# Constant-tile matrix products in TensorE's waits of the first batch, written to a PSUM bank that nobody reads

## The reference, cut to what matters

```python
n = _ln_c(x)                                   # normalise each pixel over the channels
value, query = dwconv(n, w_v), dwconv(n, w_q)  # 3x3 depthwise, stride 1
key, off     = dwconv(n, w_k, 2), dwconv(n, w_off1, 2)
pos  = tanh(gelu(layernorm(off)) @ w_off2 + ref)
v_s  = grid_sample_bilinear(value, pos)        # 784 samples per batch
attn = einsum('bcm,bcn->bmn', query, key) * SCALE
x    = x + einsum('bchw,oc->bohw', einsum('bmn,bcn->bcm', attn, v_s), w_out)
t    = tokens(x)
t    = t + sum_e gate_e(t) * (gelu(_ln_t(t) @ w1[e] + b1[e]) @ w2[e] + b2[e])   # two best of four experts
```

## Time and profile before

| what | value |
|---|---|
| median of three runs | 738.1 us (738.0, 738.1, 743.66) |
| the profiled execution | 742.88 us, span 741.0 us from first to last instruction |
| mean granted TensorE clock | 0.975 of full |
| busy: PE, DVE, ACT, POOL | 696.9, 577.5, 385.4, 216.1 us |
| the chain that ended last | PE 62%, DMA 13%, POOL 10%, ACT 6%, DVE 5% |

### The profile page before, as it was taken

One profiled execution on the slowest core, in us unless ns is written; L12 is line 12 of the kernel. 1 busy time (PEld: TensorE's weight loads), 2 busy tenths in 40 slices (PEclk: granted clock), 3 DMA queues, 4 the chain that ended last, 5 costly groups with the idle time before them and its releaser, 6 DMA issues.

```text
span 741.0 us, 9747 instructions
## 1 busy us (share of the span) xinstructions
PE 696.9 (94%) x3250; PEld 487.7 (66%) x3250; DVE 577.5 (78%) x1511; ACT 385.4 (52%) x722; POOL 216.1 (29%) x184
## 2 busy tenths in 40 slices
PE   5798998899999999899999899999998999999996
PEld 5556566566676666566766566666665665888884
DVE  4899548899999767799998277899984375677774
ACT  2313125654554626644556217544543256999995
POOL 4001700011228500111157200221285121344443
PEclk9997999799999999999999899999999999999998
DMA  9007200134565421354644522344745201121211
GB/s 191 19 0 200 55 8 1 40 70 90 99 180 118 99 48 19 69 110 102 170 120 76 95 48 47 73 86 87 206 104 109 40 25 45 47 75 48 65 47 38
DMA packets 29697, 58.71 MB, mean 79 GB/s; under 512 B 6128, under 2 KB 20176, under 8 KB 29360
## 3 DMA queue, kind: packets, MB, share of 16 engines
q0 software_dynamic: 11584, 17.90, 15.6%
q1 hardware_dynamic: 14336, 32.64, 15.2%
q10 hardware_dynamic: 3728, 7.55, 3.2%
HBM read 30.35 MB, written 14.65 MB: 61 GB/s over the span
## 4 chain that ended last, share of the span: by engine, by line
PE 62%; DMA 13%; POOL 10%; ACT 6%; DVE 5%; issue 4%; POOLq 0%; ACTq 0%
PE py L746 13%; PE pd L662 8%; POOL big L1469 8%; DMA xbuf<-ye 8%; PE ph L578 7%; PE ph L762 3%; PE ph L764 3%; PE ph L763 3%; DMA value_table<-valT 3%; PE pa L650 3%; PE pa L529 2%; PE ph L782 2%; PE ph L784 2%; PE ph L783 2%; PE py L794 2%
## 5 line engine op out<-in xcount | busy, mean ns | idle before, releaser
L746 PE MATMUL py<-hid,w 128*96 128x448 f32 x504 | 235.0, 547 | 12.3 <-ACT hid L1006 9.0
L1006 ACT ACTIVATE hid<-ph,b 128x448 f32<-128x448 f32 x252 | 159.2, 634 | 143.5 <-PE ph L764 138.9
L762 PE MATMUL ph<-x_hi,w_hi 96*128 96x448 f32 x252 | 165.2, 655 | 0.0
L1480 POOL DMA_DIRECT2D xbuf<-ye x76 | 67.6, 889 | 327.3 <-DMA xbuf<-ye 173.4
L1469 POOL DMA_INDIRECT big<-value_table,rows x64 | 85.8, 1340 | 87.0 <-DVE rows L1193 55.2
L746 PEld LDWEIGHTS py<-hid,w 128*96 128x96 f32 x504 | 81.4, 164 | 31.6 <-ACT hid L1006 13.2
L764 PE MATMUL ph<-x_hi,w_lo 96*128 96x448 f32 x252 | 93.4, 371 | 0.0
L763 PE MATMUL ph<-x_lo,w_hi 96*128 96x448 f32 x252 | 92.7, 368 | 0.0
L1416 DVE SCALAR_TENSOR_TENSOR ye<-py,b,gate_all 96x448 f32<-96x448 f32 x112 | 75.4, 675 | 11.7 <-PE py L746 6.5
L1482 POOL TENSOR_TENSOR xbuf<-xbuf,ye 96x448 f32<-96x448 f32 x36 | 54.2, 1506 | 98.9 <-DVE ye L1416 96.2
L1443 DVE TENSOR_TENSOR hid_lo<-hid,hid_hi 128x448 fp32r<-128x448 f32 x84 | 59.5, 709 | 27.8 <-ACT hid L1015 27.4
(11 more groups left out here) (165 smaller groups left out, 1052.7 us busy)
## 6 DMA issues: line engine op xcount, KB each, us to landing
gate_all<-gate_rows SPq DMA_DIRECT2D x56, 336.0 KB, 3.4
xbuf<-ye POOLq DMA_DIRECT2D x76, 168.0 KB, 3.4
value_table<-valT ACTq DMA_DIRECT2D x6, 1176.0 KB, 8.1
out<-xbuf SPq DMA_DIRECT2D x28, 168.0 KB, 2.0
xbuf<-in_x SPq DMA_DIRECT2D x3, 1176.0 KB, 10.5
value_table<-valT SPq DMA_DIRECT2D x2, 672.0 KB, 5.3
big<-value_table,rows POOLq DMA_INDIRECT x64, 2.8
value_table<-valT SPq DMA_DIRECT2D x2, 504.0 KB, 4.4
```

The lines of the kernel that those rows point to most:

```text
L746: nc.tensor.matmul(py[e % 2][0:C, 0:GPIX], w2[:, c, :], hid[:, k % 3, :], start=(j == 0), stop=(j == CPE - 1)).then_inc(hid_used, 1)
L762: nc.tensor.matmul(bank, w1_hi[:, cols], xh(b, g), start=True, stop=False)
L1006: nc.scalar.activation(hid[:, k % 3, :], ph[k % 2][:, 0:GPIX], ACT.Gelu, bias=b1[:, k % NCH:k % NCH + 1]).then_inc(hid_act, 1)
L1480: pool.dma_start(to, ye[0:C, e, :], accum_op=ALU.add).then_inc(ye_summed, 16)
```

## The change

DVE first fills a tile of ones of 128 x 224 in `hid`'s third slot. PE multiplies it with itself at eight places of batch 0: 6, 20, 5, 2, 4 products, and in `x1_back` 4, 3 and 2 behind the first three groups. Together these are 46 products. Each product is fp32 with 128 rows, 128 stationary columns and 224 moving ones, and writes into `py[1]`, where nothing reads it. PE waits for none of them; they only stand in its queue, and the first six wait for the tile of ones.

```diff
+WARM = 224
+        warm = hid[:, 2, 0:WARM]
+            def keep_busy(number):
+                for k in range(number):
+                    nc.tensor.matmul(py[1][:, 0:WARM], warm[:, 0:128], warm, start=True, stop=True)
 def head(b):
                 x_to_tokens(b)
+                keep_busy(20)
                 quarters_back(b)
 def x1_back(b, plan, chunks_to):
                     transposes(bank, [x1T[:, GRP * g + k, 0:C] for k in range(GRP)], TP, C).then_inc(dve_full, 1)
+                    if first(b) and g < 3:
+                        keep_busy(4 - g)
 def first_rest(b, plan, chunks_to):
                 off_to_channels(b)
+                keep_busy(5)
                 values_to_tokens(b, slots=range(VALUE_HALF, QT))
+                keep_busy(2)
                 offsets(b)
...
                 quarters_back(b + 1)
+                keep_busy(4)
                 x1_back(b, plan, chunks_to)
 the start of PE's program
+            pe.wait_ge(warm_ready, 1)
+            keep_busy(6)
             pe.wait_ge(ident_in, 16)
             head(0)
 the start of DVE's program
+            nc.vector.memset(warm, 1.0).then_inc(warm_ready, 1)
             nc.vector.memset(first_tiles[:, :, QUARTERS, :], 0.0)
```

More of the change, by code:

```diff
@@ L327, in build @@
         centred = sem("centred")
+        warm_ready = sem("warm_ready")
         x_part = [sem(f"x_part{n}") for n in range(len(X_PARTS))]
```

## The result

The changed kernel takes 736.24 us, the median of 20 runs, against 741.91 us for the kernel before in 20 runs. The ratio is 0.9933 with an interval of 0.9907 to 0.996: 0.7% faster, within 1% of no change. The forecast was 1.1%. The three runs from which it started had a low median; 20 put the kernel before at 741.9. The profiled execution went from 742.88 to 740.51 us, its span from 741.0 to 738.7. It is the second longest of its twenty.

The account below looks back on a forecast made before the run. PE at half clock was taken to bound the head, `key_values` (PE 1.7 us later than the samples) and the end of `x1_back`. 738.1 less 6.0 + 1.7 + 1.5, with 1.1 taken off the gain, gave 730.0 us; range 726.5 to 737.

Parts of the forecast that it names:

- The path from there to the scaled rows: Head, from the end of batch 0's `x_to_tokens`: ACT's and DVE's path keeps its 6.2 us, rows ready at 17.5.
- The twenty: Head, ahead of `quarters_back`: twenty products take 7.6 us, end at 18.95, 1.4 us longer than the gap they fill.
- no window at 0.50 in batch 0: Sign of success: no stretch of batch 0 has PE at half clock; before there were two of 10.24 us each.
- The middle: Products 5 and 2 around batch 0's offsets: PE wins 3.6 us, only the 1.7 before `key_values` waits for samples counts.
- the bound: Batch 0's `key_values`: PE's new wait of 1.9 us may bring a clock fall of its own, costing 1.7 to 3.5 us.
- `x1_back`: Products 4, then 4, 3, 2: full clock from 137.86 wins 1.8 us, less 0.3 for ACT's lateness, 1.5 net.
- The head alone: Rival, chance 0.32: gathers or a new fall at `key_values` take the middle gain, `x1_back` gives little; 731 to 735 us.
- the lift by the six: Start of the head: six products at half clock take 4.5 us and lift the clock at 5 to 6 us.
- the price of a product: All added products: two records each, 0.38 us at the full clock, 0.75 us at half clock.
- the slow rival: Rival, chance 0.07: in the head the six don't lift the clock and the twenty run at half clock; 740 to 752 us.
- transposes at the full clock: Head's `quarters_back`: transposes run at the full clock if it was up before, 4.7 us against 7.3; contrary rival 0.05.
- The sum: Whole kernel: 6.0 + 1.7 + 1.5 = 9.2 us off, less 1.1 for falls that needn't come; 738.1 becomes 730.0 us.

Follow-up runs that it names:

- e4: The kernel before, no product added, with POOL's diagonal matrices made to wait for ACT's copy of the last token slot; one execution, 752.06 us.
- e1: The changed kernel with POOL started earlier, the convolution weights' DMA having a semaphore of its own; ratio 0.9867 to the kernel before.
- e3: The changed kernel with only the first six and the twenty products, all others taken out; ratio 0.9931 to the kernel before.
- e7: The changed kernel again, without any edit, for a second profile; ratio 0.9927 to the kernel before.

## Why the prediction was too high

**The step that failed** is "The path from there to the scaled rows is ACT's and DVE's and keeps its 22.32 - 16.14 = 6.2 us". It took 20.08 - 11.73 = 8.35 us. DVE's statistics, moved up by 4.4 us, met POOL's multiplications (e4, e1). The kernel before hid that, as POOL was done 2.3 us before the statistics began; the prediction looked at what DVE and ACT wait for, and not at what runs beside them. It could have been read from the trace of the kernel before: the statistics, 4.8 us earlier, begin at 12.65, and POOL multiplies until 15.16. With POOL moved, five kernels with the head's products start their convolutions at 23.7 to 24.1 and one at 24.5, for a forecast of 23.65.

**Its consequence**: "The twenty" were not 1.4 us too long but ended 0.75 us before the rows. In the first profile the clock fell behind that wait, and the convolutions at half clock cost PE all that the head had won; in e3 and e7 it stayed up behind the same waits and 4.1 to 4.3 us were kept. What decides it in one execution was not found. The forecast "no window at 0.50 in batch 0" was wrong.

**The middle**: sized rightly in the first profile, where the third and fourth quarters of `key_values` end and `mixes` starts at 97.66 instead of 99.53, 1.9 us (forecast 1.7). DVE's samples stood still as said: their last operation ends at 96.31, before at 96.37. In e7 and e1 the bound came instead, the fall at the new wait; `mixes` alone then takes 1.7 us more. It was priced and left out of the sum. PE's rows of the kernel before, then of the changed kernel's first profile:

```profile
97.39 2.20 PE L634 MATMUL pd<-keyT,key_area 98*32 98x128 f32 x48
99.53 2.55 PE L643 MATMUL pa<-wout,kv_area 96*128 96x288 f32 x8
```

```profile
96.66 1.07 PE L643 MATMUL pd<-keyT,key_area 98*32 98x128 f32 x24 [1.36 <-DVE kv_area L1365]
97.66 2.55 PE L652 MATMUL pa<-wout,kv_area 96*128 96x288 f32 x8
```

**`x1_back`**: the wait for the gelu ends at 136.42, 1.4 us earlier, of the 1.9 brought along: ACT's lateness cost 0.4 (forecast 0.3). The products then run at the full clock, and the sixth chunk starts at 142.93 instead of 145.53: 2.6 us in all, so 0.7 of its own where 1.5 was forecast. The next transposes wait 0.48 us for DVE's `x_lo`, which PE at half clock had not to wait for.

**The rivals**: "The head alone", with 3 to 7 us of gain, came nearest. The fall at `key_values` that it names is there in e7, and e3 has the same ratio without the other twenty. Its other sentence, that in the head nothing of the kind is near, was wrong: the clock fell there too in the first profile.

**Right**: the clock of the head read from durations against its column, the lift by the six (4.42 us for them, forecast 4.5), the price of a product (twenty from 11.57 to 19.33, 7.8 us, forecast 7.6), the slow rival's low chance, and transposes at the full clock. On the last the Trainium skill ("TensorE: Matmul & The Clock Gate", Part 4) differs; in e1 all pairs take 0.33 to 0.43 us, so here the measurement decides.

**The sum** said 8.1 us of 738.1, the ratio gives 5.0. The head falls short by 1.7 to 2.0 us where the clock stays up behind the failed step (first convolution at 25.36 and 25.64, forecast 23.65), and by all 6.0 where it falls; the rest falls short at `key_values` and in `x1_back`. With POOL early, one more semaphore, it is 9.9 us of 741.04 by the ratio. That this lies near the forecast's 9.2 us is in part luck: in e1's profile 3.6 of 11.7 us are won at the first chunk and 5.2 at batch 1's key-value products; the others arise in later batches, where nothing was changed. That version is faster than the kernel before; against the changed kernel the intervals touch (0.9915 and 0.9907), though all four kernels with POOL early and all the changed kernel's products have ratios of 0.9863 to 0.9874.

## What to carry to other kernels

Before moving work earlier, lay the new times over every engine's timeline, not only over the queue of waits: two engines that never met before can hold each other up. A filled wait moves to the next place that waits for another strand, and where the clock fell because of a wait it can fall there, so look at the waits behind before filling one. The products must stand ahead of the instruction that waits, and their worth is in what runs right behind. Where the clock falls differs between executions of one kernel, so take a second profile before explaining a fall.

## What was not expected of the hardware

- A POOL multiplication of 128 x 1152 holds up DVE operations for up to its whole 2.1 us. In e4 even a one-input operation of 28 elements (TENSOR_SCALAR) took 2.14 us, while in the kernel before and the changed one the batch statistics beside the same POOL work kept their 0.74 to 0.80 us a group.
- In the kernel before, 10.75 us of back-to-back token products at half clock do not raise the clock; in the changed kernel, once raised by the six, it stays up through 6 us of them.
- After waits of 0.7 and 1.04 us the clock fell in one execution and not in two others of the same stretch.
